# Local attention layers: scores and output products issued for two slots at a time, ScalarE's and VectorE's work ordered anew, six value buffers

## The reference, cut to what matters

```python
def attn_layer(x, Wqkv, qs, ksc, Wo):            # 16 heads of 64
    q, k, v = heads_of(x @ Wqkv)
    q, k = l2norm(q) * qs, l2norm(k) * ksc
    q, k = rotary(q) * scale, rotary(k) / scale
    # windows of 32 queries see their own and the previous window (64 keys)
    sim = einsum(q, k_two_windows) * 8.0, masked to 0 <= i - j <= 32
    return (softmax(sim) @ v_two_windows) @ Wo
for i in range(6):
    x = attn_layer(shift_tokens(x), ...) + x
    x = ffn_layer(shift_tokens(x), ...) + x       # layernorm, a * gelu(gate), W2
```

## Time and profile before

| | us |
|---|---|
| median of 3 runs | 2557.08 (2556.41 to 2559.36) |
| the profiled execution, its own time | 2557.28 |
| its span, first to last instruction | 2555.5 |
| TensorE busy | 2406.9 (94%) |
| VectorE busy | 2006.4 (79%) |
| ScalarE busy | 1885.0 (74%) |
| GpSimd busy | 1766.4 (69%) |

### The profile page before, as it was taken

One profiled execution on the slowest core, in us unless ns is written; L12 is line 12 of the kernel. 1 busy time (PEld: TensorE's weight loads), 2 busy tenths in 40 slices (PEclk: granted clock), 3 DMA queues, 4 the chain that ended last, 5 costly groups with the idle time before them and its releaser, 6 DMA issues.

```text
span 2555.5 us, 98078 instructions
## 1 busy us (share of the span) xinstructions
PE 2406.9 (94%) x36442; PEld 1706.3 (67%) x36442; DVE 2006.4 (79%) x4388; ACT 1885.0 (74%) x6630; POOL 1766.4 (69%) x1605
## 2 busy tenths in 40 slices
PE   7999778879999999999999999999999999789999
PEld 6888544446666666666666666666667666368874
DVE  5555699978888888888888888888888888565644
ACT  4777788858888888888888888888888888533323
POOL 2888886468888888888888888888888888222200
PEclk9999999999999999999999999999999999899999
DMA  4111210021112111111112111211111111100000
GB/s 122 15 15 16 50 13 12 10 77 36 33 34 61 38 42 33 52 48 41 33 33 67 41 33 34 62 38 41 34 53 48 41 33 34 32 1 1 1 1 17
DMA packets 177876, 91.06 MB, mean 36 GB/s; under 512 B 40974, under 2 KB 174328, under 8 KB 177408
## 3 DMA queue, kind: packets, MB, share of 16 engines
q1 hardware_dynamic: 168574, 80.42, 11.7%
q0 software_dynamic: 8192, 4.21, 1.4%
...
q10 hardware_dynamic: 642, 0.15, 0.0%
...
## 4 chain that ended last, share of the span: by engine, by line
PE 81%; DVE 11%; issue 4%; POOL 2%; ACT 1%; SPq 0%; DMA 0%; DVEq 0%; POOLq 0%; ACTq 0%
PE bank L1170 13%; PE bank L1187 9%; PE scores L1222 7%; PE bank L1233 7%; PE bank L1177 6%; PE scores L1204 6%; DVE rg_prod L1008 3%; PE bank L1159 3%; PE bank L1262 3%; PE bank L1280 2%; PE bank L1271 2%; PE bank L639 2%; PE scores L1198 2%; PE scores L671 1%; PE bank L1904 1%
## 5 line engine op out<-in xcount | busy, mean ns | idle before, releaser
L1606 POOL TENSOR_TENSOR rs<-ssc,neg_half 128x8 f32<-128x8 f32 x384 | 643.5, 1676 | 41.3 <-DVE ssc L1426 41.3
L1596 POOL TENSOR_TENSOR t_pair<-qn_pair,tabs 128x512 f32<-128x512 f32 x384 | 488.8, 1273 | 12.3 <-DVE qn_pair L1414 11.6
L1534 ACT ACTIVATE pr<-scores,negmax 128x64 f32<-128x64 f32 x1536 | 460.3, 311 | 49.3 <-DVE negmax L1434 24.2
L1586 POOL TENSOR_TENSOR pr<-pr,rec 128x256 f32<-128x256 f32 x384 | 235.1, 612 | 282.9 <-DVE rec L1406 282.9
L1170 PE MATMUL bank<-wqk,xs 128*128 128x512 f32 x768 | 402.6, 606 | 12.9 <-DVE qn_pair L1414 11.7
L1069 POOL DMA_INDIRECT rg_win<-rg_images,share_down x256 | 258.6, 1010 | 90.2 <-issue 57.6
L1534 ACT ACTIVATION_READ_ACCUMULATOR pr<-scores,negmax 128x1 f32 x1536 | 311.3, 203 | 0.0
L1422 DVE TENSOR_REDUCE ss<-sq 128x8 f32<-128x512 f32 x384 | 261.1, 680 | 33.4 <-ACT sq L1557 32.4
L1414 DVE TENSOR_TENSOR qn_pair<-bank,rs 128x512 f32<-128x512 f32 x384 | 257.5, 671 | 27.2 <-POOL rs L1606 27.1
L1525 ACT COPY vt<-bank 128x256 f32<-128x256 f32 x361 | 135.1, 374 | 187.8 <-issue 187.7
L1387 DVE TENSOR_TENSOR qr_pair<-t_pair 128x512 f32<-128x512 f32 x384 | 266.2, 693 | 0.3 <-issue 0.2
...
## 6 DMA issues: line engine op xcount, KB each, us to landing
rg_prod<-vt SPq DMA_DIRECT2D x1536, 32.0 KB, 1.9
...
rg_win<-rg_images,share_down POOLq DMA_INDIRECT x256
...
```

The source lines that it names most:

```text
L1534: ex = act.activation(pr[t % 2][:, h * BAND:(h + 1) * BAND], sl_ps[:, h // 2, h % 2 * BAND:(h % 2 + 1) * BAND], ACT.Exp, bias=negmax[t % 2 ...
L1596: pool.tensor_tensor(t2[t % 2][:, :].rearrange("p (i h f e) -> p i h f e", i=2, h=GH, f=2), qn[t % 2][:, :].rearrange("p (i h f e) -> p i ...
L1606: pool.tensor_tensor(rs[t % 2][:, :], ssc[t % 2][:, :], neg_half[:, 0:8], ALU.pow)\
```

## The change

Units are paired. TensorE runs `score` for units u - 7 and u - 6 in one go, then `attend` for u - 11 and u - 10, in every second slot (odd u), and `project` for the pair in the slot after. The mask matmuls cover both units: two instructions of 256 columns instead of four of 128. The two banks hold four score tiles in columns 0 to 255 and four output tiles in 256 to 511. VectorE takes the maxima of both units in one reduction, in the slot after the scores and ahead of `cosines`; ahead of it stands a wait for the copy of the pair's outputs. ScalarE copies the outputs of a pair in one instruction at the head of its even slots. Its order in even slots is: output copy, squares, probability copy, exponentials; in odd slots: half the exponentials, probability copy, the other half, squares. The value copy moves to the end of the slot in which the values are made (slot 7), the shifted state is copied one slot earlier, into three buffers. There are three `qkT`, four `pr`, six `vt` and four `vx` buffers; the four DMAs per unit stay, and the reloads of the weights on their queue move with the units. All lags grow: `L_PROJ`, and with it the start of the FFN chunks and `TAIL`, by two slots.

```diff
...
-L_QKV, L_ROPE, L_COS, L_SUM, L_TURN, L_SCORE, L_V, L_MOVE, L_EXP, L_PROB, L_PROJ = 1, 2, 3, 4, 5, 6, 5, 6, 7, 8, 9
+L_QKV, L_ROPE, L_COS, L_SUM, L_TURN, L_V, L_EXP, L_REC, L_PROB, L_PROJ = 1, 2, 3, 4, 5, 7, 8, 9, 10, 11
+L_SCORE, L_ATTEND, L_OUT = 7, 11, 12
...
-LATER = {0: (1, 2), 1: (2, 1), 8: (10, 0), 9: (10, 1)}
...
-        sl_ps, ol_ps = scores[:, :, 0:P], scores[:, :, P:2 * P]
+        sl_ps = scores[:, :, 0:2 * P].rearrange("p r (i k) -> p r i k", i=2)
+        ol_ps = scores[:, :, 2 * P:4 * P].rearrange("p c (i n) -> p c i n", i=2)
...
-        xs = [sb(f"xs{i}", [P, P]) for i in range(2)]
+        xs = [sb(f"xs{i}", [P, P]) for i in range(3)]
...
-        vx = [rg_flat[1][:, 6 * CW + i * GV:6 * CW + (i + 1) * GV] for i in range(2)]
+        vx = [rg_flat[1][:, 6 * CW + i * GV:6 * CW + (i + 1) * GV] for i in range(4)]
...
+        qkT_local = qkT + [e_spare[:, 13 * F:14 * F]]
+        vt_local = [v[:, :] for v in vt] + [e_spare[:, 14 * F + i * GV:14 * F + (i + 1) * GV] for i in range(2)]
+        pr_local = [pr[i % 2][:, i // 2 * GB:(i // 2 + 1) * GB] for i in range(4)]
...
-                    near, far = vt[t % 3], vx[t % 2]
+                    near, far = vt_local[t % 6], vx[t % 4]
...
-                    sp.wait_ge(a.o_ready, TICKS + t - 1)
+                    if t >= 4:
+                        sp.wait_ge(a.o_ready, TICKS + t - 3)
...
-                l, g = (t + 4) // TICKS + 1, (t + 4) % TICKS - TICKS + GROUPS
+                l, g = (t + 6) // TICKS + 1, (t + 6) % TICKS - TICKS + GROUPS
...
-                    sp.wait_ge(a.qk_ready, TICKS + t + 5)
+                    sp.wait_ge(a.qk_ready, TICKS + t + 7)
...
+        def pair_at(u, lag):
...
+            return (u - lag, u - lag + 1) if (u - lag) % 2 == 0 and live(u - lag) else None
...
+        def through(t):
...
+            return TICKS + min(max(t, 0), LOCAL)
...
+            def score(pair_, u):
+                pe.wait_ge(a.qkT_moved, TICKS + pair_[1] + 1)
...
+                    pe.matmul(sl_ps[:, r, :, :].rearrange("p i (a k) -> p (i a) k", a=2), ident16[:, :],
+                              over(local_mask[:, :], [P, 4, BAND], 1), start=True, stop=False, skip_group_check=True)
+                for t in pair_:
+                    st = qkT_local[t % 3]
+                    for pair in range(2):
+                        for key, lo in BLOCKS:
+                            for r in range(2):
+                                row = slice(r * HD, (r + 1) * HD)
+                                mm = pe.matmul(sl_ps[lo:lo + WINDOW, r, t % 2, pair * BAND:(pair + 1) * BAND],
+                                               st[row, pair * P + lo:pair * P + lo + WINDOW],
+                                               st[row, (2 + pair) * P + key:(2 + pair) * P + key + BAND],
+                                               start=False, stop=True, skip_group_check=True)
+                mm.then_inc(a.sc_ready, 2)
...
+            def attend(pair_):
+                pe.wait_ge(a.pT_moved, TICKS + pair_[1] + 1)
+                for t in pair_:
+                    pe.wait_ge(a.v_spread[t % 2], 64 * (t // 2 + 1))
+                    for k, (_, lo, hi) in enumerate(SPANS):
...
+                            for pair in range(2):
+                                row = slice(pair * HD, (pair + 1) * HD)
+                                at = SLOT_V[k][pair] * P + r * HD
+                                values = vt_local[t % 6] if k == 2 * pair else vx[t % 4]
+                                mm = pe.matmul(ol_ps[r * HD:(r + 1) * HD, pair, t % 2, lo:hi], values[row, at:at + HD],
+                                               pT[t % 2][row, r * P + lo:r * P + hi],
+                                               start=True, stop=True, skip_group_check=True)
+                mm.then_inc(a.o_ready, 2)
...
+            def tiles(u):
+                scored, attended = pair_at(u, L_SCORE), pair_at(u, L_ATTEND)
+                if scored or attended:
+                    pe.wait_ge(a.exp_ready, through(u - L_SCORE))
+                    pe.wait_ge(a.oT_moved, through(u - L_ATTEND))
+                if scored:
+                    score(scored, u)
+                if attended:
+                    attend(attended)
...
-                for t in projections(u, 0):
-                    project(t)
...
-                for t in projections(u, 1):
-                    project(t)
...
-                if live(u - L_SCORE):
-                    score(u - L_SCORE, u)
-                if live(u - L_PROB):
-                    attend(u - L_PROB, u)
-                for t in projections(u, 2):
+                tiles(u)
+                for t in pair_at(u, L_OUT) or ():
...
-            def maximum(t, u):
-                if live(t):
-                    dve.wait_ge(a.sc_ready, TICKS + t + 1)
-                    if live(u - L_PROB):
-                        dve.wait_ge(a.o_ready, TICKS + u - L_PROB + 1)
-                    dve.wait_ge(a.exp_ready, TICKS + t - 1)
-                    dve.tensor_reduce(negmax[t % 2][:, :].rearrange("p (r a) -> p r a", r=2),
-                                      sl_ps.rearrange("p r (a k) -> p r a k", a=2), AX.X, ALU.max, negate=True)\
-                        .then_inc(a.negmax_ready, 1)
+            def maximum(u):
+                scored = pair_at(u, L_SCORE)
+                if scored:
+                    dve.wait_ge(a.sc_ready, TICKS + scored[1] + 1)
+                    dve.wait_ge(a.oT_moved, through(u - L_ATTEND + 2))
+                    dve.wait_ge(a.exp_ready, TICKS + scored[0])
+                    dve.tensor_reduce(negmax_pair[:, :].rearrange("p (r i a) -> p r (i a)", r=2, i=2),
+                                      sl_ps.rearrange("p r i (a k) -> p r (i a) k", a=2), AX.X, ALU.max, negate=True)\
+                        .then_inc(a.negmax_ready, 2)
...
-                add(u - 1 - L_PROJ)
+                add(u - L_OUT)
...
+                maximum(u - 1)
...
-                    normed(u - L_ROPE)
-                    inverse(u - L_EXP)
...
-                    inverse(u - L_EXP)
-                    normed(u - L_ROPE)
+                inverse(u - L_REC)
+                normed(u - L_ROPE)
...
+                    dve.wait_ge(a.sc_ready, TICKS + t - 2)
+                    dve.tensor_copy(qkT_local[t % 3][:, :], turn_ps[:, :]).then_inc(a.qkT_moved, 1)
...
+                    dve.wait_ge(a.o_ready, TICKS + t - 5)
+                    dve.tensor_copy(vt_local[t % 6], vl_ps).then_inc(a.v_moved, 1)
...
-                maximum(u - L_SCORE, u)
...
+            def shifted(b):
+                if live(b * GROUPS):
+                    if b >= B:
+                        act.wait_ge(s.lf_state, (b - B) // CH + 1)
+                    if b >= 3:
+                        act.wait_ge(a.v_ready, TICKS + (b - 2) * GROUPS)
+                    shift(xs[b % 3], ZT[:, b % B * P:(b % B + 1) * P], s.xs_ready)
...
+            def exponentials(u, mine):
...
+                    act.wait_ge(a.pT_ready, TICKS + max(t - 3, 0))
...
+                    for h in mine:
+                        col = h // 2 * GH + t % 2 * 2 + h % 2
+                        ex = act.activation(pr_local[t % 4][:, h * BAND:(h + 1) * BAND],
+                                            sl_ps[:, h // 2, t % 2, h % 2 * BAND:(h % 2 + 1) * BAND],
+                                            ACT.Exp, bias=negmax_pair[:, col:col + 1],
...
+                    if GH - 1 in mine:
+                        ex.then_inc(a.exp_ready, 1)
...
+            def pT_copy(u):
...
+            def squares(u):
...
+            def slot(u):
+                attended = pair_at(u, L_OUT)
+                if attended and not bursts(u - 1):
+                    b, g = attended[0] // GROUPS, attended[0] % GROUPS
+                    act.wait_ge(a.o_ready, TICKS + attended[1] + 1)
+                    if g == 0:
+                        act.wait_ge(a.y_ready, B + max(attended[0] - GROUPS, 0))
+                    act.copy(oT[b % 2][:, g * GV:(g + 2) * GV].rearrange("p (i c n) -> p i c n", i=2, c=2),
+                             ol_ps.rearrange("p c i n -> p i c n")).then_inc(a.oT_moved, 2)
+                if (u - L_EXP) % 2 == 0:
+                    squares(u)
+                    pT_copy(u)
+                    exponentials(u, range(GH))
+                else:
+                    exponentials(u, range(GH // 2))
+                    pT_copy(u)
+                    exponentials(u, range(GH // 2, GH))
+                    squares(u)
...
+                    act.wait_ge(a.sc_ready, TICKS + max(t - 2, 0))
+                    act.copy(qkT_local[t % 3][:, :], turn_ps[:, :]).then_inc(a.qkT_moved, 1)
+                t = u - L_V
+                if live(t) and not bursts(u):
+                    act.wait_ge(a.v_ready, TICKS + t + 1)
+                    act.wait_ge(a.o_ready, TICKS + max(t - 5, 0))
+                    act.copy(vt_local[t % 6], vl_ps).then_inc(a.v_moved, 1)
+                if u == 0:
```

(5 more changed lines are left out.)

108 lines of the change are left out of this document (15 added, 93 removed).

## The result

The changed kernel takes 2573.7 us (2568.2 to 2578.9, five runs), the kernel before 2557.5 (2556.4 to 2562.5, five runs on the same chip): ratio 1.006, interval 1.0041 to 1.0078. Forecast were 2467 us, a ratio of 0.965. The change makes the kernel a little slower; the gain is missing by 107 us. The profiled execution of the changed kernel has a span of 2566.4 us and a mean granted clock of 0.988.

What follows compares the result with a forecast made beforehand. TensorE's own work was taken to fill 97% of a 69.0 us round; 65.0 after gives -90 us over 22.4 rounds, -4 for early slots, +4 for the longer pipeline: 2467 us, range 2426 to 2520.

Steps and rivals of the forecast that it cites:

- the FFN steps: Sixteen slots of an FFN chunk, paired from 0+1 to 14+15; their products put pairs between 7.3 and 8.9 us.
- 0.3 added: Per round, 0.3 us for two slots in which an engine has the batch's shift or GpSimd the FFN's power.
- scores 0.39 + 0.25: TensorE's scores of a pair: 0.39 us for the first unit's 32 instructions, 0.25 for the second's.
- the entry of 0.15: TensorE's cost of entering another array shape before output products, 0.15 us, paid once in two slots after the change.
- the Gelu pair: Pair of FFN steps 10+11, where Gelu and its table loads take ScalarE 4.4 us: forecast 8.9 us.
- so 7.3: Loop from output products through ScalarE's queue to masks, scores and output products, closing last in pairs with little FFN: 7.3 us.
- one such wait, 0.4: Pair of FFN steps 12+13: the value product waits 0.4 us for the probability copy behind the squares.
- GpSimd: unchanged, 56.6: GpSimd's busy time in a round of 16 slots stays at 56.6 us after the change.
- grouping gives nothing: Rival, chance 0.06: shape entries are part of each TensorE instruction's price; round 67.5 us, -33 us, 2524 us.
- the 60 cycles a matmul: Trainium skill's overhead for every TensorE matmul, however few columns; 0.80 us for 32, weighed as speaking against the change.
- waits eat half: Rival, chance 0.16: VectorE held at `maximum` until the output copy, 0.25 us more idleness a pair; round 67, 2512 us.
- The slower rival: Chance 0.06: second loop through ScalarE's late squares and VectorE, 7.1 us, decides from 8.63 a pair; 8.9 gives 2606 us.

Runs made afterwards that it cites:

- e14: Changed kernel with VectorE's turned-query sum and cosines reading one input (sine part, cosine table left out) and every second head's output products left out: ratio 0.9837 to kernel before.
- e1: Changed kernel with VectorE's turned-query sum and cosine products as one-input reductions, sine part and cosine table left out: ratio 0.9964 to kernel before.

## Why the prediction was wrong

Pair by pair (us, units t mod 16; the FFN steps as in the prediction; changed kernel at its 20th percentile):

| units | steps | predicted | changed kernel | e14 |
|---|---|---|---|---|
| 0, 1 | 6, 7 | 7.97 | 8.61 | 8.14 |
| 2, 3 | 8, 9 | 8.39 | 8.61 | 8.53 |
| 4, 5 | 10, 11, Gelu | 8.9 | 8.92 | 8.89 |
| 6, 7 | 12, 13 | 7.9 | 8.61 | 8.60 |
| 8, 9 | 14, 15 | 8.39 | 8.54 | 8.53 |
| 10, 11 | 0, 1 | 8.39 | 8.54 | 8.53 |
| 12, 13 | 2, 3 | 7.46 | 8.09 | 8.08 |
| 14, 15 | 4, 5 | 7.3 | 7.77 | 7.76 |
| round | | 64.7 | 67.69 | 67.03 |

The forecast round was 65.0 with 0.3 added; the mean measured is 69.41. The 4.4 us between them, times the prediction's 22.4 rounds, are 99 of the missing 107 us. They are, by the steps of the prediction:

- **"scores 0.39 + 0.25"**: the first failed step. Grouping was to save the entry of 0.15, and it does, but the second 32 instructions take 0.40 and not 0.25. 0.15 us in each of the five pairs that TensorE fills: 0.75.
- **The FFN's steps**: `F_UP` is 11, so the up products stand in steps 11 to 13, not 10 to 12, as the section on the kernel before and the prediction have it. The pair of steps 12 and 13 (units 6, 7) has one product more than I gave it, and TensorE fills it: 0.55 beside the scores' 0.15. The number of products in a round was right; one moved out of the Gelu pair, where ScalarE hid it.
- **The loops, "so 7.3"**: bare pairs close in 7.77 and not 7.3, the one with the variance in 8.09 and not 7.46: 1.1 us a round. The chain closed before the masks; TensorE waits earlier, before its value product, which `values` holds back until the probability copy is done. One bare pair, TensorE's pieces and ScalarE's copies:

```profile
1412.45 0.60 PE L1183 MATMUL bank<-ident,qr_pair 128*128 128x128 f32 x4
1413.12 0.67 PE L1245 MATMUL bank<-wv,xs 128*128 128x256 f32 x2
...
1416.80 0.60 PE L1183 MATMUL bank<-ident,qr_pair 128*128 128x128 f32 x4
1417.74 0.67 PE L1245 MATMUL bank<-wv,xs 128*128 128x256 f32 x2 [0.34 <-issue]
```

```profile
1412.65 0.37 ACT L1546 COPY pT<-bank 128x256 f32<-128x256 f32 x1 [0.54 <-PE bank L1165]
...
1417.28 0.37 ACT L1546 COPY pT<-bank 128x256 f32<-128x256 f32 x1
```

  In both slots the values start 0.1 us after the copy's end, 0.23 and 0.50 us later than the next piece follows such transposes elsewhere (0.11 us behind the start of the last). That is 0.73 of the 0.95 us between 7.77 and TensorE's 6.82. The prediction had one such wait, 0.4, and only in the pair of steps 12 and 13, where TensorE's products cover it.
- **"GpSimd: unchanged, 56.6"**: the second failed step. It counted GpSimd's instructions and not what VectorE does while they run. Moving `maximum` behind the addition brought two-input instructions onto the power and the rotation: GpSimd 60.0 a round. 0.66 us in every round (67.69 against e14's 67.03; e1 alone has 67.08), and 25 us of time by e1. The trace of before had the sign, 33 powers of 2.1 us among 384.
- **Not in the sum at all**: the instruction stops, 1.0 us a round by the holes counted, 33 us of time by e14 against e1, which is more than the holes hold; why is open. Against the number of instructions the prediction weighed only their rate on the array.

These make 0.75 + 0.55 + 1.1 - 0.3 = 2.1 for the regular part without collisions, 0.66 for the regular collisions, and 69.41 - 67.69 = 1.72 for the irregular slots, 4.5 together.

What was right: masks, output products and projections in their places and nearly to size; the entry of 0.15 us as a cost of changing shape and not of count (so the rival "grouping gives nothing", and with it the 60 cycles a matmul, is out); the Gelu pair, 8.92 for 8.9; `maximum` 0.69 for 0.70; DMAs, since no wait for one stands before an output product. The rival "waits eat half" had the right kind of thing, idleness on VectorE, at half the size, and the wrong place: before `maximum` VectorE stands 42 us in the whole kernel, 0.22 a pair, and before `normed`, for the stretched power, 109. The slower rival (0.06) had the right sign with the wrong cause: its second loop through late squares does not appear, and no pair passes the 8.63 us that it needed but the Gelu pair. The range left no room for a cost that no row of the prediction shows, and the stops and the collisions were such.
